# Attention in beats of two steps: the order of scores, maxima, value products and side work in a four-layer sequence kernel

## The reference

```python
# layers 0, 1, 2 (with their own weights; layer 1 also normalises q and k per head)
h = modulate(layernorm(x), shift, scale)                  # shift, scale, gate from silu(c) @ W
q, k, v = split(h @ w_qkv + b_qkv)                        # 16 heads of 9 channels
o = softmax(q k^T / sqrt(9)) v
x = x + gate * (o @ w_proj + b_proj)
x = x + gate2 * mlp(modulate(layernorm(x), shift2, scale2))   # 144 -> 576 -> 144, gelu
#   layer 0: four expert mlps, the best two of each token weighted by softmax
# layer 3
U = qr(P)                                                  # P is 144 x 64
R = expm(A(c))                                             # antisymmetric 64 x 64, per sequence
out = x + ((x U) R - x U) U^T
```

## Time and profile before

| | |
|---|---|
| median of 3 runs | 1089.74 us |
| the profiled execution | 1085.88 us, its span 1083.8 us |
| TensorE matmul busy | 864.2 us, 80% of the span |
| VectorE busy | 663.1 us, 61% |
| ScalarE busy | 385.4 us, 36% |
| GpSimd busy | 163.3 us, 15% |
| mean granted TensorE clock | 0.663 |

### The profile page before, as it was taken

The page is one execution under the profiler, slowest core; times in us unless marked ns, Lnnn a source line. Parts: engine busy times, 40 slices in busy tenths (PEclk is TensorE's granted clock), DMA queues, the critical chain, the costliest instruction groups (busy, mean ns, idle before and its releaser), DMA issues.

```text
span 1083.8 us, 11314 instructions
## 1 busy us (share of the span) xinstructions
PE 864.2 (80%) x3551; PEld 454.6 (42%) x3551; DVE 663.1 (61%) x2080; ACT 385.4 (36%) x682; POOL 163.3 (15%) x351
## 2 busy tenths in 40 slices
PE   5665888896897669798777887879897789989856
PEld 1432343233673333366444344545343444335425
DVE  4378777677536887853577667565666554564232
ACT  0311343232451433345234332325332355435412
POOL 4201013101041000213401003011003010002020
PEclk9999965555796655679865555855555765558556
DMA  3000001000021000002100000000000000000000
GB/s 105 15 1 6 17 11 36 9 15 1 13 56 47 1 0 1 1 17 67 44 0 1 1 1 15 13 1 1 1 1 10 19 1 1 1 0 1 5 6 11
DMA packets 18108, 14.95 MB, mean 14 GB/s; under 512 B 3295, under 2 KB 15479, under 8 KB 18050
## 3 DMA queue, kind: packets, MB, share of 16 engines
q1 hardware_dynamic: 18002, 14.22, 4.9%
q10 hardware_dynamic: 48, 0.02, 0.0%
HBM read 13.62 MB, written 0.61 MB: 13 GB/s over the span
## 4 chain that ended last, share of the span: by engine, by line
PE 59%; DVE 32%; issue 4%; ACT 2%; POOL 2%; DMA 0%; DVEq 0%; SPq 0%; POOLq 0%; ACTq 0%
PE o_bank L1266 11%; PE m_bank L1245 11%; DVE row_max L809 8%; PE d_bank L1384 4%; PE s_bank L1234 3%; PE d_bank L1327 3%; PE m_bank L1425 3%; PE m_bank L1253 2%; PE d_bank L1371 2%; PE d_bank L1216 2%; PE d_bank L1298 2%; DVE h_tok L868 2%; PE d_bank L1283 1%; PE d_bank L1284 1%; DVE q_rows L1056 1%
## 5 line engine op out<-in xcount | busy, mean ns | idle before, releaser
L652 ACT ACTIVATE probs<-s_bank 128x512 f32<-128x512 f32 x384 | 220.5, 596 | 487.8 <-PE s_bank L1234 484.9
L809 DVE TENSOR_REDUCE row_max<-m_bank 128x1 fp32r<-128x512 f32 x384 | 256.0, 686 | 154.4 <-PE m_bank L1245 149.0
L1245 PE MATMUL m_bank<-k_t,q_t 32*128 32x512 f32 x384 | 213.9, 741 | 63.0 <-DVE q_rows L1056 23.0
L1234 PE MATMUL s_bank<-q_t,k_t 32*128 32x512 f32 x384 | 236.3, 736 | 5.8 <-ACT probs L652 5.0
L1266 PE MATMUL o_bank<-probs,v_aug 128*32 128x512 f32 x768 | 175.7, 1005 | 3.9 <-DVE o_tok L827 3.2
L1245 PEld LDWEIGHTS m_bank<-k_t,q_t 32*128 32x128 f32 x384 | 80.4, 267 | 183.7 <-issue 64.8
L1234 PEld LDWEIGHTS s_bank<-q_t,k_t 32*128 32x128 f32 x384 | 89.2, 267 | 30.7 <-ACT probs L652 15.9
L578 POOL TENSOR_TENSOR h_tok<-h_tok,mod 128x144 f32<-128x144 f32 x48 | 24.0, 499 | 265.6 <-DVE h_tok L868 265.6
L1425 PE MATMUL m_bank<-q_rows,ident 64*64 64x144 f32 x128 | 44.7, 449 | 18.0 <-DVE q_rows L1056 17.9
L1384 PE MATMUL d_bank<-w_f,g_f 128*128 128x144 f32 x384 | 55.0, 286 | 0.0
L1384 PEld LDWEIGHTS d_bank<-w_f,g_f 128*128 128x128 f32 x384 | 50.1, 189 | 2.1 <-ACT g_f L719 2.1
(11 more groups left out here) (224 smaller groups left out, 1362.6 us busy)
## 6 DMA issues: line engine op xcount, KB each, us to landing
raw_a<-in_L_cond_w_dram SPq DMA_DIRECT2D x10, 288.0 KB
w_f<-in_L_cond_w_dram SPq DMA_DIRECT2D x10, 288.0 KB
w_rows<-in_L_cond_W_dram SPq DMA_DIRECT2D x8, 141.8 KB
raw_d<-in_L_cond_w_dram SPq DMA_DIRECT2D x30, 36.0 KB
x_tok<-in_x_dram SPq DMA_DIRECT2D x2, 288.0 KB, 4.2
raw_a<-in_L_cond_W_fc_dram SPq DMA_DIRECT2D x2, 288.0 KB
w_f<-in_L_cond_W_fc_dram SPq DMA_DIRECT2D x2, 288.0 KB
out_dram<-moe SPq DMA_DIRECT2D x4, 144.0 KB, 1.9
```

Of the source, the lines that this page charges most:

```text
L652: act.activation(probs[:, n % PROBS, :], s_banks[n % S_BANKS][:, :], ACT.Exp, scale=HD ** -0.5)\
L809: dve.tensor_reduce(row_max[:, grp % 2, t, MAXROW + 32 * j:MAXROW + 32 * j + 1], bk[:, :], AX.X, ALU.max).then_inc(drained, 1)
L1234: pe.matmul(s_banks[n % S_BANKS][:, :], k_t[rows, par, g, kt * P:(kt + 1) * P], q_t[rows, par, g, :], start=True, stop=True).then_inc(s["s ...
L1245: pe.matmul(bk[:, :], q_t[rows, par, g, t * P:(t + 1) * P], k_t[rows, par, g, :], start=True, stop=True).then_inc(s["max_full"], 1)
```

## The change

Two steps become one beat (`PAIR` = 2), so there are 192 beats, 8 to a group. In a beat TensorE issues two maximum scores and then both scores; `pv`, `max_turn`, the stage slots and the solver parts come behind them. The plans are recomputed in beats at the same rates. The order of the maximum tiles (`MAX_ORDER`) is such that the two maxima directly ahead of two scores use the two other row groups. The value product of a key tile comes one step later (in the first beat of a group ahead of everything). `MAX_SHARE` is 2, 4, 2, 2, 2, 2, 2, 0 for the beats of a group, and `o_turn` comes in the second beat, between its first two maxima and its last two. ScalarE does `o_copy` ahead of the group's first two exponentials.

```diff
+PAIR = 2
+BEATS = STEPS // PAIR
+GBEATS = GSTEPS // PAIR
...
-        first, last = (0 if block == 0 else 4), (STEPS if block == BLOCKS - 1 else STEPS - GSTEPS - 2)
+        first, last = (0 if block == 0 else 2), (BEATS if block == BLOCKS - 1 else BEATS - GBEATS - 1)
...
-        plan[2 * i + 1].append(part)
+        plan[i].append(part)
     for i, part in enumerate(QR_CHAIN[EARLY:]):
-        plan[i * QR_PACE // 2].append(part)
+        plan[i * QR_PACE // 4].append(part)
     for i, part in enumerate(EXP_CHAIN):
-        plan[EXP_FROM + 4 * i].append(part)
+        plan[EXP_FROM + 2 * i].append(part)
...
-MAX_SHARE = [2, 2] + [1] * (GSTEPS - 4) + [0, 0]
-TURN_AT = GSTEPS - 2
+MAX_SHARE = [2, 4] + [2] * (GBEATS - 3) + [0]
+TURN_AT = GBEATS - 1
+MAX_ORDER = [(0, 2), (0, 3), (0, 0), (0, 1), (1, 0), (1, 1), (1, 2), (1, 3),
+             (2, 0), (2, 1), (2, 2), (2, 3), (3, 0), (3, 1), (3, 2), (3, 3)]
... ScalarE
-                if n % GSTEPS == 3 and n > GSTEPS:
-                    o_copy(n // GSTEPS - 1)
+                if beat % GBEATS == 0 and beat:
+                    o_copy(beat // GBEATS - 1)
+                exps(PAIR * beat)
+                exps(PAIR * beat + 1)
... VectorE
-                    fill[0] = fill_once
-                    for _ in range(SLOTS[n - 1]):
-                        next(woven)
+                    for i in range(slots):
+                        if i == slots - 1:
+                            fill[0] = fill_once
+                        next(woven)
+                    fill[0] = fill_once
...
+                if at == 1 and grp > 0:
+                    while len(maxima) > PAIR:
+                        next_max()
+                    o_normalise(grp - 1)
... TensorE
-            for n in range(BLOCKS * STEPS):
-                grp = n // GSTEPS
-                if grp + 1 < BLOCKS * G:
-                    for t, j in max_tiles(n):
-                        max_scores(grp + 1, t, j)
+            for beat in range(BLOCKS * BEATS):
+                grp, at = divmod(beat, GBEATS)
+                n = PAIR * beat
+                maxima = list(max_tiles(beat)) if grp + 1 < BLOCKS * G else []
+                if at == 0 and grp > 0:
+                    pv(n // GRP - 1)
+                while len(maxima) > PAIR:
+                    max_scores(grp + 1, *maxima.pop(0))
+                if at == 1 and grp > 0:
+                    o_turn(grp - 1)
+                for tile in maxima:
+                    max_scores(grp + 1, *tile)
                 scores(n)
-                if n % GSTEPS == 4 and grp > 0:
-                    o_turn(grp - 1)
-                if n % GRP == 2 and n > GRP:
+                scores(n + 1)
+                if at == TURN_AT and grp + 1 < BLOCKS * G:
+                    max_turn(grp + 1)
+                if n % GRP == 0 and at > 0:
                     pv(n // GRP - 1)
-                if n % GSTEPS == TURN_AT and grp + 1 < BLOCKS * G:
-                    max_turn(grp + 1)
-                for _ in range(SLOTS[n]):
+                for _ in range(SLOTS[beat]):
                     next(woven)
-                for part in SOLVER_PLAN[n]:
+                for part in SOLVER_PLAN[beat]:
                     solver(part)
```

More of the change, by code:

```diff
@@ L126, with slot_beats @@
         "mlp": (1, 1), "rotate": (1,)}
-def slot_steps():
-    steps = [0] * (BLOCKS * STEPS)
+def slot_beats():
+    beats = [0] * (BLOCKS * BEATS)
     for block in range(BLOCKS):
-        first, last = (0 if block == 0 else 4), (STEPS if block == BLOCKS - 1 else STEPS - GSTEPS - 2)
+        first, last = (0 if block == 0 else 2), (BEATS if block == BLOCKS - 1 else BEATS - GBEATS - 1)
         room = [w for st in stages(block) for w in ROOM[st[0]]]
         for i in range(len(room)):
-            steps[block * STEPS + first + sum(room[:i]) * (last - first) // sum(room)] += 1
-    return steps
-SLOTS = slot_steps()
+            beats[block * BEATS + first + sum(room[:i]) * (last - first) // sum(room)] += 1
+    return beats
+SLOTS = slot_beats()
 V_CHAIN = [("v", t) for t in range(VT)] + [("v_rows",)]
@@ L153 @@
 QR_PACE = 5
-EXP_FROM = 141
+EXP_FROM = 70
 def solver_plan():
-    plan = [[] for _ in range(BLOCKS * STEPS)]
+    plan = [[] for _ in range(BLOCKS * BEATS)]
     for i, part in enumerate(V_CHAIN):
-        plan[2 * i + 1].append(part)
+        plan[i].append(part)
     for i, part in enumerate(QR_CHAIN[EARLY:]):
-        plan[i * QR_PACE // 2].append(part)
+        plan[i * QR_PACE // 4].append(part)
     for i, part in enumerate(EXP_CHAIN):
-        plan[EXP_FROM + 4 * i].append(part)
+        plan[EXP_FROM + 2 * i].append(part)
     last = {part: n for n, parts in enumerate(plan) for part in parts}
-    assert last[EXP_CHAIN[-1]] < last[("less_one",)] and last[QR_CHAIN[-1]] < BLOCKS * STEPS - GSTEPS
+    assert last[EXP_CHAIN[-1]] < last[("less_one",)] and last[QR_CHAIN[-1]] < BLOCKS * BEATS - GBEATS
+    assert all(sum(part in chain for part in parts) <= 1 for parts in plan for chain in (QR_CHAIN, EXP_CHAIN))
     return plan
@@ L186, with max_tiles @@
 SOLVER_BANK = ("v_rows", "p_load", "mgs", "lu", "skew", "taylor", "turned", "square", "y", "m")
-MAX_SHARE = [2, 2] + [1] * (GSTEPS - 4) + [0, 0]
-TURN_AT = GSTEPS - 2
-def max_tiles(step):
-    at = sum(MAX_SHARE[:step % GSTEPS])
-    return [divmod(i, GRP) for i in range(at, at + MAX_SHARE[step % GSTEPS])]
+MAX_SHARE = [2, 4] + [2] * (GBEATS - 3) + [0]
+TURN_AT = GBEATS - 1
+MAX_ORDER = [(0, 2), (0, 3), (0, 0), (0, 1), (1, 0), (1, 1), (1, 2), (1, 3),
+             (2, 0), (2, 1), (2, 2), (2, 3), (3, 0), (3, 1), (3, 2), (3, 3)]
+def max_tiles(beat):
+    at = sum(MAX_SHARE[:beat % GBEATS])
+    return MAX_ORDER[at:at + MAX_SHARE[beat % GBEATS]]
 class Banks:
@@ L1164, in _ @@
             woven = side(WOVEN)
-            for n in range(BLOCKS * STEPS + 1):
-                grp = n // GSTEPS
-                if n % GSTEPS == 5 and grp > 0:
-                    o_normalise(grp - 1)
-                maxima = list(max_tiles(n)) if grp + 1 < BLOCKS * G else []
+            for beat in range(BLOCKS * BEATS + 1):
+                grp, at = divmod(beat, GBEATS)
+                maxima = list(max_tiles(beat)) if grp + 1 < BLOCKS * G else []
                 def next_max():
@@ L1240, in max_scores @@
                 rows = slice(32 * j, 32 * j + 32)
-                if grp % G == 0 and t == 0 and j == 0:
+                if grp % G == 0 and (t, j) == MAX_ORDER[0]:
                     for w in stacks[grp // G]:
```

44 lines of the change are left out of this document (24 added, 20 removed).

## The result

The changed kernel takes 1105.17 us (median of 4 runs, 1100.83 to 1108.64), the kernel before 1089.34 in the same runs (1077.64 to 1089.98): a ratio of 1.017, 95% interval 1.009 to 1.025. It is slower, by 1 to 2.5%. The forecast was 1068, and the time lies above the range, near the third rival's 1110. In all that follows medians are of every run, while ratios and their intervals leave out runs more than 1.5% above the fastest of the same kernel in the set, which is why the two can differ.

A forecast was written before the change was run, and what follows sets the result against it. No single engine bounds it: TensorE and VectorE hand the critical path to each other. Stage joints -15.8, solver joints -10.9, the turn +10.8 and the ring -6 sum to -21.9 us, forecast 1068 us, range 1037 to 1098.

The forecast's parts named there:

- third rival: Scores queue behind a beat's second maximum, waiting for VectorE; +15 to +25 us, 1110 us, chance 0.19.
- the turn: Start of each group: second beat's fourth maximum delays transposes; 0.9 us in 12 groups, +10.8 us; bounds -0.8 to +2.2 each.
- the ring: Three banks for maxima and parts: maxima no longer wait for parts; -6 us, bounds 0 and 20 lost back.
- solver joints: Joined pairs formerly split by solver parts only: nothing for 25 in groups 0 to 7, half counted for 35 lu: -10.9 us.
- How many pairs are joined: Odd steps followed by TensorE side work gain: 96 of 192, 36 with a stage, 60 with only a solver part.
- the price of a batch: Four products on TensorE cost the same as a pair, 0.72 us, or 0.43 at high clock; a joint saves 0.62.
- Stage joints: 36 joined pairs formerly split by a stage: 23 save 0.62 us, five 0.3, eight nothing; -15.8 us.
- The mlp beats: Expert steps: the wait for VectorE's moe disappears, but ScalarE's gelu table load is late next; 0 us.
- the rest: Copy ahead of exponentials, GpSimd and DMA order: nothing, or 0.6 us a group if the copy doesn't fit.
- Slower: Scores and value product queue behind the second maximum: 51 us at turns, 20 of ring waits, less joints; 1110 us, chance 0.19.
- The drain of the banks decides: Batches everywhere wait for the last exponential or reduction; joints' 10 to 15 us lost at turns; 1087 to 1091 us, chance 0.14.

The follow-up runs named there:

- lean pair: Kernel before and changed kernel, both with the solver left out nearly whole: 899.72 and 935.10 us.
- exp_first: Changed kernel with the exponential part ahead of the QR part in beats that have both: 1090.48 us, ratio 1.016.
- sf_exp: Changed kernel with solver parts ahead of the stage slots, and the exponential part ahead of the QR part: 1069.11 us, ratio 0.995.
- lean kernels: Kernel before and changed kernel, solver left out nearly whole, with 16 maximum tiles a group (899.72, 935.10 us) or 14 (895.76, 884.87 us).
- before_sf: Kernel before with the solver's parts ahead of the stage slots on every engine: 1054.34 us, ratio 0.976.
- solver_first: Changed kernel with the solver's parts ahead of the stage slots on every engine: 1071.28 us, ratio 0.991.
- lean14_after: Changed kernel, solver left out nearly whole, 14 maximum tiles a group instead of 16, two in each of the first seven beats: 884.87 us.
- lean_after: Changed kernel with the solver left out nearly whole: 935.10 us, ratio 0.871 to the kernel before.
- lean_before: Kernel before with the solver left out nearly whole: 899.72 us, ratio 0.831 to the full kernel before.
- lean14_before: Kernel before, solver left out nearly whole, 14 maximum tiles a group instead of 16, one in each of 14 steps: 895.76 us.

## Why the prediction was wrong

The sum said -21.9 us, and the medians differ by +15.8. Two of its steps failed: the turn, counted too small, and the ring, counted with the wrong sign. The half that I counted for the solver joints went with the ring.

*How many pairs are joined, and the price of a batch.* Right: batches of four start together (925.45 to 925.46), and TensorE's busy time fell by 49 us where I had counted 60. The mean clock that I took from the page was too high: it shows full clock for the first 88.9 us, of which more below. From 160 us on it is 0.61, full clock for 22% and not a third, so a joint is worth 0.66 us and not 0.62. That changes no sign.

*Stage joints, -15.8 us.* Neither borne out nor refuted. In the lean pair, where little else moves, groups 2, 5, 10 and 17, all with stages, are 4.2, 3.3, 2.5 and 4.9 us shorter, 14.9 together; the clock was higher in three of them. Other groups with stages are longer (4 and 8, by 2.1 and 1.7 us). And of groups 1, 2 and 12 to 14, which I had 1 to 3 us shorter in the changed kernel, only 2 is (6.3); 12 and 13 are 3.2 and 5.1 longer.

*Solver joints, -10.9 us.* Wrong. Groups 11 and 15, lu and exponential parts beside attention, went from 28.9 to 31.7 and from 31.7 to 32.4 us. The half I counted is nothing in the order as changed. With the exponential part first it is there: group 11 takes 27.4 us in `exp_first` and `sf_exp`, 1.5 less than before although it pays a turn. For mgs I had said nothing is gained, and that held, but group 3's 25.7 to 27.3 is outside the 1 us I allowed: it, too, pays for the turn, as far as can be told.

*The turn, +10.8 us.* The first step that failed. The mechanism was the right one (the fourth maximum waits for a reduction, the transposes start at 2.3 us: it was 2.35; the group at 20 to 21 us: 21.1; no first score waits for `q_t`: the next one starts at 946.54 right behind the value product). The price of the bank came out by luck: I read 1.57 us from a maximum (920.67) queued behind a score that waited for ScalarE (920.61), so it doesn't show when the bank was free; 1.64 is what the wait came to (925.45 to 927.09). The size was not right: 1.25 us in group 19, not 0.9, and not only in the 12 groups in which TensorE sets the pace, since group 3 pays too (1.6). But not in every group either: group 7 went from 28.7 to 28.3 us at the same clock. My bound of +2.2 was the better guess in the lean kernels, where the two tiles cost 46 us more joined than before, 2.1 for each of 22 turns, the clock's part included. I compared the new second beat with nothing: the rows that I had not read were the old turn's, in which the value product covers the surplus reductions. I priced "the first score no longer waits" and "the fourth maximum waits" as two edits, though the same value product was moved from the one place to the other.

*The ring, -6 us.* The second, wrong in sign: the waits for `lu` went to 41.0 us. My own bound had it: where an exponential part makes four takes, the second maximum waits for the QR part with both scores behind it, "20 lost back"; the waits for `lu` grew by 24.5. I had not counted that joining doubles such beats (23 for 11 with an `lu` part), nor that a stage ahead of the part on VectorE makes each wait long (6.96 us at 568.52). The other two signs in this place failed as well: waits for `q_rows` stayed (23.0, then 23.6), and those for `row_max` fell (16.6, then 13.6). What the order of the two parts is worth lies between the 5.6 us of groups 11 and 15 and the 15 us of `exp_first`'s median.

*The mlp beats, 0, and the rest, 0.* No run tested them. Waits of L1386 for `g_f` went from 1.5 us in 2 waits to 9.0 in 6, late next as I had written.

*The sum again.* -15.8 for the stages, +1.25 x 22 = +27.5 for the turns, nothing for the solver joints: +12 us, against +13.6 between the profiled spans of `before_sf` (1056.5) and `solver_first` (1070.1), and 16.9 by medians. That comes near and proves little, since by groups the terms don't show as they should: at 0.50 in both, group 3 is 1.6 and group 11 2.7 us longer, groups 7 and 2 are 0.4 and 2.3 shorter. For the kernel as changed (+15.8) the ring's cost and what beats with stages gain weren't told apart.

*The rivals.* "Slower" had both places, and I gave it 0.19 because its longest waits stood in a long norm. But what decides is not the longest wait, it is how many there are. Its 1110 us near the measured 1105 is luck: its own terms, 51 and 20 less 15.8 and 10.9, make +44 us, 1134, and not the +15 to +25 that I wrote. "The drain of the banks decides" was the same mechanism seen in the wrong place. The Trainium skill ("TensorEngine Tiling (Array Packing)", section "PSUM Bottleneck"), quoted there, says that packing leaves the evacuation as it was; the rows agree: one reduction takes 0.69 us in the kernel before and in the changed one, and `lean14_after`, with 46 reductions fewer, is 50 us under `lean_after`. The Trainium skill ("Perfetto Trace Analysis", section "Identifying Performance Opportunities") says of a gap that comes back on an engine that it can mean too few PSUM buffers for the next tile; the 0.41 and 0.35 us ahead of L1260 in group 19 are such gaps, the second in every key tile; a ring of four banks was not run.

Open: a whole kernel with no surplus in its second beat was not run, since all 16 tiles need a place in seven beats. Whether joining then pays on top of `before_sf` isn't shown; in the lean kernels it is worth 11 us. The clock's share stays open too, and so does which loss, the turn's or the ring's, is the larger in the changed kernel.

## What to carry to other kernels

When products are packed closer, the ring that drains them keeps its pace: count the reductions that fall between two pieces of covering work, before and after, and look at what a moved product used to cover. Where an engine serves a chain and a long stage in one turn of the loop, try the chain first: that order gave 30 us here in the one kernel and 33 in the other, more than any batching. And when an edit repairs a slow variant, put it into the old kernel as well before you call it the cause.

## What the runs showed of the hardware

The same instructions took very different times by the granted clock. In `lean_before` a group of attention alone took 19.8 us at 0.50 (group 19) and 15.57 at 0.80 (group 15); in `lean14_after` 19.52 at 0.50 and 14.76 at 0.85. In `lean14_before` TensorE was busy for 19.05 of group 15's 19.82 us and stayed at 1.2 GHz. Full clock came in other groups from profile to profile: group 19, with the same instructions, took 19.8 us at 0.50 in the kernel before and 16.4 at 0.74 in `before_sf`. What decides it, no run here shows; the mean clock doesn't order the times either (the kernel before took 1065.69 us at 0.639 and 1069.38 at 0.676).

The clock at the start of a profile is not to be trusted. In the kernel before, the head and group 0 are shown at 1.00. Group 0 takes 36.70 us there with TensorE busy for 24.95; in `before_sf` it is shown at 0.50, takes 35.70 and is busy for 25.09, with the same 83 products. Twice the clock at the same busy time can't be, so the 1.00 is likely what is shown while nothing has been recorded. It lifts the mean of a whole span (0.663 against 0.624 in the two; by an estimate, half of the clock too much is worth 0.02 of 1083.8 us over group 0 alone and 0.06 over the head as well), which is why stretches behind it are compared here.
